# Batch 1's convolution as a step of the order, silu(z) with a place per batch, fewer root steps on GpSimd, and a new order of all engines

## What is computed

```python
# mixer: context (4,256,128), z = layernorm(x) (4,256,256)
x1 = silu(conv4(in_proj(ctx)) + conv_b)            # 256 channels
dt_low, B, C = split(x_proj(x1))                   # 8, 16, 16
dt = softplus(dt_proj(dt_low) + dt_b); A = -exp(A_log)
state = state * exp(dt*A) + (dt*x1) * B            # scan over 256 positions, 16 states a channel
y = (sum_n state*C + D*x1) * silu(z)
x = x + y
# feed-forward, on layernorm(x)
bitlinear(v, w, b) = act_quant(rms_norm(v)) @ weight_quant(w).T + b
h = gelu(silu(bitlinear(v, w1, b1)))               # 1024 wide
x = x + bitlinear(layer_norm(h, g, b), w2, b2)
```

## Time and profile before

| what | value |
|---|---|
| runs of the kernel (us) | 204.31, 201.55, 202.54; median 202.54 |
| profiled execution, span from its first to its last instruction | 201.9 us |
| its own device time | not given apart from the span; the fastest run is 0.35 us under the span, the median 0.6 us over it |
| mean granted TensorE clock | 0.890 of full speed |
| table loads on ScalarE | 28 |

### The profile page before, as it was taken

One profiled execution on the slowest core, in us unless ns is written; L12 is line 12 of the kernel. 1 busy time (PEld: TensorE's weight loads), 2 busy tenths in 40 slices (PEclk: granted clock), 3 DMA queues, 4 the chain that ended last, 5 costly groups with the idle time before them and its releaser, 6 DMA issues.

```text
span 201.9 us, 3382 instructions
## 1 busy us (share of the span) xinstructions
PE 161.6 (80%) x1161; PEld 121.8 (60%) x1167; DVE 164.1 (81%) x249; ACT 161.2 (80%) x262; POOL 142.9 (71%) x139
## 2 busy tenths in 40 slices
...
GB/s 176 292 93 364 413 419 101 3 203 206 10 208 9 97 114 0 187 220 21 148 60 0 109 104 153 58 26 0 0 3 0 0 0 26 28 28 3 11 25 70
DMA packets 20193, 20.13 MB, mean 100 GB/s; under 512 B 13448, under 2 KB 16976, under 8 KB 19536
## 3 DMA queue, kind: packets, MB, share of 16 engines
...
...
## 4 chain that ended last, share of the span: by engine, by line
ACT 24%; PE 24%; POOL 17%; DVE 17%; issue 14%; DMA 1%; DVEq 0%; POOLq 0%; ACTq 0%
ACT dA L692 10%; DVE st L1006 7%; POOL st L847 7%; PE ps L512 4%; PE ps L588 4%; PE ps L451 3%; PE ps L551 3%; DVE stats L1076 3%; PE ps L612 2%; POOL sm L874 2%; PE ps L619 2%; POOL sm L872 2%; ACT w_raw L729 2%; POOL sm L876 1%; PE ps L480 1%
## 5 line engine op out<-in xcount | busy, mean ns | idle before, releaser
L847 POOL TENSOR_TENSOR st<-st,bc 128x1024 f32<-128x1024 f32 x32 | 75.5, 2372 | 19.2 <-DVE st L1006 18.9
L1006 DVE TENSOR_TENSOR_SCAN st<-dA,ps 128x1024 f32<-128x1024 f32 x32 | 72.3, 2276 | 7.5 <-PE ps L512 6.1
L692 ACT ACTIVATE dA<-dt,negA 128x255 f32<-128x255 f32 x128 | 53.2, 498 | 0.2
L512 PE MATMUL ps<-diagB,dtuT 64*128 64x128 f32 x512 | 44.8, 306 | 4.9 <-DVE st L1006 3.5
L512 PEld LDWEIGHTS ps<-diagB,dtuT 64*128 64x128 f32 x512 | 34.9, 198 | 18.1 <-issue 9.5
L551 PE MATMUL ps<-id_f,st 128*128 128x128 f32 x256 | 35.2, 288 | 2.3 <-POOL st L847 2.3
L551 PEld LDWEIGHTS ps<-id_f,st 128*128 128x128 f32 x256 | 29.8, 147 | 5.8 <-POOL st L847 3.0
L612 PE MATMUL ps<-id_f,w_raw 128*128 128x128 f32 x64 | 11.7, 343 | 14.0 <-POOL w_raw L911 8.9
L612 PEld LDWEIGHTS ps<-id_f,w_raw 128*128 128x128 f32 x64 | 9.9, 181 | 15.4 <-issue 13.9
L588 PE MATMUL ps<-rows_sb,diag 128*128 128x512 f32 x32 | 17.2, 663 | 0.4 <-ACT w_raw L725 0.4
L761 ACT ACTIVATE q2T<-ps 128x1024 bf16<-128x1024 f32 x8 | 8.1, 1013 | 10.4 <-PE ps L612 10.4
...
## 6 DMA issues: line engine op xcount, KB each, us to landing
...
w_raw<-w2T SPq DMA_DIRECT2D x1, 1024.0 KB, 12.3
...
```

Source lines behind the costliest of these rows:

```text
L512: mm = nc.tensor.matmul(o[:, i:i + SG // 2, t, r, :], dtuT[rows, b % 2, h, t, :], diagB[rows, b % 2, t, n, :], start=True, stop=True)
L692: e = nc.scalar.activation(dA[:, k % DA_RING, i * L + 1:(i + 1) * L], dt[:, h, b % 2, 1:L], ACT.Exp, scale=negA[:, h, n:n + 1])
L847: tt(s, s, bc[:, ng].rearrange("p s l -> p (s l)"), ALU.mult).then_inc(prod_done, 1)
L1006: nc.vector.tensor_tensor_scan(st[:, k % ST_RING, :], dA[:, k % DA_RING, :], slot(k), 0.0, ALU.mult, ALU.add).then_inc(scanned, 1)
```

## The change

Batch 1's convolution, `turn_half(0)`, `scale_b(0)` and `scale_rest(0)` become steps of `PE_AT`; the first writes bank 2 instead of bank 0, batch 2's bank 3 instead of 2, with their own waits. `silu_z` writes a buffer of its own for each batch and no longer waits for `z_turned`. GpSimd's `root1` and `root2b` fold the factor 127/1e-5 into the number whose root is taken and have two steps instead of three; `root2a` leaves out its third step for tiles 4 to 7. `out_scale`, `quant1` and `wmean` use the other scale. ScalarE's table loads are written out, by the set last loaded. All four tables are new.

```diff
...
 VECTOR_AT = (
+    "z_norm:1 spread_b:1 spread_b:2 spread_b:3",
+    "dt_half:1",
+    "",
     "dt_neg:1",
+    "dt_mask:1 wmean:0",
+    "",
+    "dt_sum:1",
+    "",
+    "dt_neg:2",
     "dt_mask:2",
     "gate:0 gate:1 x1:0 x1:1",
+    "",
+    "ln1:0 dt_sum:2",
+    "quant1:0",
+    "",
+    "dt_neg:3 clip_weights:0 clip_weights:1",
+    "dt_mask:3",
+    "dt_sum:3 bn2:0",
+    "",
+    "gate:2 gate:3 x1:2 x1:3 gain:0 ln1:1",
+    "",
     "quant1:1",
+    "",
+    "amax2:0",
+    "scales2:0",
+    "bn2:1 bn2:2",
+    "gate:4 gate:5 x1:4 x1:5 gain:1",
+    "",
+    "gain:2 amax2:1 scales2:1 ln1:2",
+    "amax2:2 bn2:3 scales2:2",
+    "res:0 quant1:2 gain:3",
+    "",
+    "amax2:3 bn2:4 gain:4 scales2:3 gate:6 gate:7 x1:6 x1:7 res:1 ln1:3 res:2 quant1:3 amax2:4 bn2:5 scales2:4 "
+    "gain:5 amax2:5 bn2:6 scales2:5 gain:6 res:3 bn2:7 amax2:6 gain:7 scales2:6 res:4 amax2:7 scales2:7 res:5 "
+    "res:6 res:7",
 )
 SCALAR_AT = (
     "silu_u:1",
     "copy_xd:1",
+    "",
+    "",
+    "sum_weights:0 dt_bias:1",
+    "copy_half:1 sum_weights:1 dt_exp:1",
+    "silu_z:0 silu_u:2",
     "copy_xd:2",
+    "copy_du:1",
     "dt_bias:2",
     "dt_exp:2",
     "copy_z:0",
+    "silu_z:1 scale_weights:0 silu_u:3",
+    "copy_xd:3",
     "",
     "copy_du:2",
     "dt_bias:3",
+    "copy_q1:0",
+    "scale_weights:1 dt_exp:3",
+    "",
+    "silu:0 copy_z:1 gelu:0 silu_z:2 silu_z:3 copy_du:3 silu:1 norm:0",
+    "copy_z:2",
+    "copy_z:3 square:0",
+    "",
+    "",
+    "",
     "copy_q1:1",
+    "silu:2 gelu:1 gelu:2 scale2:0",
+    "copy_q2:0 norm:1",
+    "",
+    "norm:2 square:1 silu:3 gelu:3 scale2:1 square:2",
+    "copy_q2:1 scale2:2 norm:3 copy_q2:2",
+    "copy_q1:2 silu:4 gelu:4 square:3 silu:5 gelu:5 scale2:3 square:4 copy_q2:3 copy_q1:3 silu:6 gelu:6 "
+    "square:5 silu:7 gelu:7 square:6 copy_q2:4 copy_q2:5 square:7 copy_q2:6 copy_q2:7",
 )
 POOL_AT = (
+    "z_root:0",
+    "",
     "",
     "",
     "dt_series:1",
+    "",
+    "",
     "",
     "",
     "dt_series:2",
     "",
     "",
+    "root1:0 add_b2:0",
+    "",
+    "",
     "dt_series:3",
     "",
+    "root2a:0",
+    "",
+    "shift:0 add_b2:1 root1:1 root2b:0",
+    "",
+    "",
+    "",
+    "out_scale:0",
+    "",
+    "root2a:1 root2a:2",
+    "shift:1",
+    "root2b:1 shift:2 out_scale:1 root1:2",
+    "root2b:2 root2a:3",
+    "",
     "shift:3",
     "",
+    "root2a:4 root2b:3 add_b2:2 out_scale:2 out_scale:3 root1:3 add_b2:3 root2b:4 out_scale:4 root2a:5 "
+    "scale_last:4 root2b:5 root2a:6 out_scale:5 scale_last:5 root2a:7 root2b:6 scale_last:6 root2b:7 "
+    "scale_last:7 out_scale:6 out_scale:7",
 )
 PE_AT = (
+    "convolve:2 convolve:3 turn_half:0 xdbl:1 scale_b:0 scale_rest:0 scale_b:1 dtraw:1 convolve:4 scale_b:2 "
+    "scale_rest:1 scale_rest:2 convolve:5",
+    "turn_half:1 scale_b:3 scale_rest:3 scale_b:4 scale_rest:4",
+    "wsum:0",
+    "scale_b:5 scale_rest:5",
+    "scale_b:6 xdbl:2 scale_rest:6 scale_b:7 scale_rest:7 turn_du:1",
+    "dtraw:2 scale_b:8 scale_rest:8",
+    "scale_b:9 scale_rest:9",
+    "turn_z:0 scale_b:10",
+    "scale_rest:10 scale_b:11 scale_rest:11 convolve:6 convolve:7",
+    "scale_b:12 xdbl:3 scale_b:13",
+    "scale_rest:12",
+    "turn_du:2",
+    "scale_rest:13 scale_b:14 dtraw:3 scale_rest:14 turn_q1:0",
+    "scale_b:15 scale_rest:15 scale_b:16 scale_rest:16 turn_z:1 bias:0",
+    "",
+    "mm1:0 scale_b:17 scale_rest:17 bias:1 scale_b:18",
+    "scale_rest:18 turn_du:3 mm1:1 turn_z:2 scale_b:19 scale_rest:19 scale_b:20 scale_rest:20",
+    "turn_z:3",
+    "",
+    "scale_b:21 scale_rest:21 scale_b:22 scale_rest:22 turn_q1:1",
+    "bias:2 scale_b:23 scale_rest:23 mm1:2",
+    "scale_b:24 scale_rest:24 scale_b:25 scale_rest:25",
+    "",
+    "",
+    "turn_q2:0 scale_b:26 scale_rest:26 scale_b:27 bias:3 scale_rest:27",
+    "mm1:3 scale_b:28 scale_b:29 scale_rest:28 scale_rest:29",
+    "",
+    "mm2:0 turn_q2:1 scale_b:30 scale_rest:30",
+    "turn_q2:2 scale_b:31 scale_rest:31 turn_q1:2 bias:4 mm1:4 bias:5",
+    "mm1:5",
+    "",
+    "",
+    "mm2:1 mm2:2 turn_q2:3 turn_q1:3 bias:6 mm1:6 mm2:3 bias:7 turn_q2:4 mm1:7 turn_q2:5 mm2:4 mm2:5 turn_q2:6 "
+    "turn_q2:7 mm2:6 mm2:7",
 )
...
         def xin(b):
-            return bank(0) if b == 1 else bank(2)
+            return bank(3) if b == 2 else bank(2)
...
-            held = {"big": (diagB_done, GROUPS), "low": (scanned, UNITS - 1), "high": (scanned, UNITS)}
+            held = {"big": (u_ready, NB), "low": (scanned, UNITS - 1), "high": (scanned, UNITS)}
...
                 if i == HALVES:
                     pe.wait_ge(in_ctx, 16)
                     pe.wait_ge(taps_scaled, 1)
-                elif h == 0:
-                    take("big", u_ready, b + 1)
+                    pe.wait_ge(u_ready, 1)
+                elif i == 2 * HALVES:
+                    pe.wait_ge(diagB_done, GROUPS)
+                elif i == 3 * HALVES:
+                    pe.wait_ge(u_ready, 2)
...
             b_cols()
-            for i in range(HALVES, 2 * HALVES):
-                convolve(i)
-            pe.wait_ge(in_id, 16)
-            turn_half(0)
-            scale_b(0)
-            scale_rest(0)
...
             def silu_z(b):
                 act.wait_ge(z_small, 4)
-                if b:
-                    act.wait_ge(z_turned, b)
                 for h in range(HALVES):
                     j = h * NB + b
-                    nc.scalar.activation(siluz[:, h, :], x_nat[:, h, b, :], ACT.Silu,
+                    nc.scalar.activation(siluz[:, b, h, :], x_nat[:, h, b, :], ACT.Silu,
...
             def root2a(t):
...
-                pool.wait_ge(root2a_step, 3 * t + 2)
-                ts(s[:, 2:3], mv2[:, t % 2, 0:1], s[:, 1:2], -1.0, ALU.mult, ALU.mult).then_inc(root2a_step, 1)
+                if t < LAST:
+                    pool.wait_ge(root2a_step, 3 * t + 2)
+                    ts(s[:, 2:3], mv2[:, t % 2, 0:1], s[:, 1:2], -1.0, ALU.mult, ALU.mult).then_inc(root2a_step, 1)
...
             def root2b(t):
...
-                tt(s[:, 5:6], s[:, 4:5], m_half[:, 0:1], ALU.pow).then_inc(root2b_step, 1)
-                pool.wait_ge(root2b_step, 3 * t + 2)
-                ts(s[:, 6:7], s[:, 5:6], LEVELS / EPS, None, ALU.mult).then_inc(root2b_step, 1)
+                tt(s[:, 6:7], s[:, 4:5], m_half[:, 0:1], ALU.pow).then_inc(root2b_step, 1)
...
+            dt_neg(0)
             z_norm(0)
-            dt_neg(0)
...
```

More of the change, by code:

```diff
@@ L54 @@
 VECTOR_AT = (
-    "spread_b:1 spread_b:2 dt_half:1",
-    "spread_b:3",
+    "z_norm:1 spread_b:1 spread_b:2 spread_b:3",
+    "dt_half:1",
+    "",
     "dt_neg:1",
+    "dt_mask:1 wmean:0",
     "",
-    "z_norm:1 dt_mask:1 wmean:0 dt_sum:1",
+    "dt_sum:1",
     "",
-    "dt_neg:2 clip_weights:0",
+    "dt_neg:2",
     "dt_mask:2",
+    "gate:0 gate:1 x1:0 x1:1",
+    "",
[8 more added lines that the diff above has]
+    "",
+    "quant1:1",
+    "",
[11 more added lines that the diff above has]
+    "res:6 res:7",
+)
+SCALAR_AT = (
+    "silu_u:1",
+    "copy_xd:1",
+    "",
[3 more added lines that the diff above has]
+    "silu_z:0 silu_u:2",
+    "copy_xd:2",
+    "copy_du:1",
+    "dt_bias:2",
+    "dt_exp:2",
+    "copy_z:0",
+    "silu_z:1 scale_weights:0 silu_u:3",
+    "copy_xd:3",
+    "",
+    "copy_du:2",
+    "dt_bias:3",
+    "copy_q1:0",
[4 more added lines that the diff above has]
+    "copy_z:3 square:0",
     "",
@@ L65 @@
     "",
-    "gate:0 gate:1 x1:0 x1:1",
-    "dt_sum:2 ln1:0",
-    "quant1:0 dt_neg:3 clip_weights:1",
-    "",
[L70 to L89, removed]
-)
[L91 to L102, removed]
+    "copy_q1:1",
+    "silu:2 gelu:1 gelu:2 scale2:0",
+    "copy_q2:0 norm:1",
+    "",
+    "norm:2 square:1 silu:3 gelu:3 scale2:1 square:2",
+    "copy_q2:1 scale2:2 norm:3 copy_q2:2",
+    "copy_q1:2 silu:4 gelu:4 square:3 silu:5 gelu:5 scale2:3 square:4 copy_q2:3 copy_q1:3 silu:6 gelu:6 "
+    "square:5 silu:7 gelu:7 square:6 copy_q2:4 copy_q2:5 square:7 copy_q2:6 copy_q2:7",
+)
+POOL_AT = (
+    "z_root:0",
     "",
@@ L105 @@
     "",
[L106 to L111, removed]
-    "",
-    "",
[L114 to L127, removed]
-POOL_AT = (
-    "",
-    "",
-    "dt_series:1",
-    "z_root:0",
+    "dt_series:1",
+    "",
+    "",
     "",
@@ L167 @@
-    "scale_rest:3 convolve:5",
-    "scale_b:4 scale_b:5 wsum:0 scale_rest:4 scale_rest:5 xdbl:2",
-    "turn_du:1",
-    "convolve:6 scale_b:6 dtraw:2 scale_b:7 scale_rest:6 scale_rest:7",
-    "convolve:7",
-    "",
-    "turn_z:0 scale_b:8 scale_rest:8 scale_b:9 scale_rest:9",
-    "scale_b:10 scale_rest:10 scale_b:11",
-    "scale_rest:11 scale_b:12 xdbl:3",
-    "",
-    "scale_rest:12 turn_du:2 scale_b:13 dtraw:3",
-    "scale_rest:13 scale_b:14 turn_q1:0 bias:0 scale_rest:14",
-    "mm1:0 turn_z:1 scale_b:15 scale_rest:15",
@@ L539, in sum_states @@
                         pe.wait_ge(diag_D_done, HALVES)
-                        pe.wait_ge(u_ready, 2)
                     elif h == 0:
```

126 lines of the change are left out of this document (48 added, 78 removed).

## The result

The changed kernel takes 217.88 us (median of four runs, 215.45 to 218.88) against 202.56 us; the ratio is 1.0706, with a 95% interval of 1.061 to 1.080. Every ratio here is one of means, taken without the runs that lie over 1.5% above the fastest of their kernel, and so differs a little from the quotient of the medians (1.0756 here). The forecast was 195.0 us. The direction was wrong, and the time lies outside the range.

A forecast was written before the change was run, and what follows sets the result against it. No engine alone was taken as the bound; the order decides, with everything hanging from VectorE's 32 scans. Span 201.9 - 4.5 - 2.1 - 0.9 = 194.4 us, plus 0.6 gives a forecast of 195.0 us, range 190.0 to 201.5.

The forecast's parts named there:

- The new order of the scans: First to last scan: the reordered tables cut VectorE's waits, its work unchanged at 119.5 us; 4.5 us saved.
- Its standing: VectorE's waits between scans: 6.4 us instead of 10.9, of which 1.8 us allowed for handovers.
- the small steps: Root steps on GpSimd: long ones are held up beside VectorE's two-input instructions, so the next small step would be too.
- The cold clock: Rival: TensorE stands in rows 16 to 23 and its clock falls, 9.4 us lost, run 204.4; chance 0.07.
- ScalarE ahead of `bn2:0`: Rival: late ScalarE holds `bn2:0`, scan 17 and all behind it; gain only 3.5 us, run 199.0; chance 0.22.
- Start: Before the first scan: moving batch 1's convolution gains nothing; scan 0 at 24.1 us, as before.
- Loads: ScalarE's table loads: 26 instead of 28, 2.6 us off ScalarE.
- Root steps: GpSimd's shorter root steps on the chain of the end: 1.4 us counted, 0.9 taken; 2.9 if the long times were their own.
- After the last scan: ScalarE's last row: earlier pieces bring tile 6's `silu` to +15.9 us from +18.9; 2.1 of 3 us taken.
- From span to run: Whole kernel: 0.6 us added to the span, which stood that far below the runs' median of 202.54.
- the sum: Whole span: 201.9 less 4.5 (scans), 2.1 (after the last scan) and 0.9 (root steps) gives 194.4 us.

The follow-up runs named there:

- e10: e1 with GpSimd's step `root1:0` moved behind the product of unit 11 instead of in front of it; 202.74 us, ratio 0.9904.
- e1: The changed kernel's new code with all four tables of the kernel before (the old order); 199.74 us, ratio 0.986 to the kernel before.
- e3: The changed kernel with GpSimd's product by C left out and four one-column powers in its place; 191.91 us, ratio 0.9465.
- e4: The changed kernel with each GpSimd product cut into four instructions of 128x256; 207.88 us, ratio 1.0246.
- e5: The changed kernel with four groups of GpSimd's steps put in front of their products; 217.18 us, ratio 1.0665.
- e6: The kernel before with the change's shorter root steps alone; 200.53 us, ratio 0.9838.

## Why the prediction was wrong

- **The step that failed** is the first of "The new order of the scans": "VectorE's work up to the last scan is the same set in both orders (119.5 us)". The set is the same and its time is not. From the first scan to the last scan's end VectorE was busy 118.4 us before and 143.4 us after. A duration from the trace of before was a duration in that order, with GpSimd kept away. The hand count put each product at the end of its scan, beside the side steps, and took both at their lengths. What the runs show in its place: a meeting with a product under way adds up to 2.1 us to a VectorE instruction (2.0 in e10), 24.4 us in the whole kernel, and goes with the order (e1) and with the products (e3).
- **Its standing was forecast well**: 6.4 us expected between scans, and VectorE's timeline after has waits of 1.86, 0.21, 1.28, 0.83 and 1.12, 5.3 us. What made the scans late was the stretches: scan 6 starts at 49.41 instead of the forecast 44.5, and L959, L1139 and L972 ahead of it took 2.0, 1.8 and 2.0 us too much.
- **The prediction had the mechanism in its hand**, and only for the small steps: "I read this as GpSimd held up, so the next small step will be held up in its place." It worked in one direction. The opposite one, VectorE held up by a product of 2.37 us, was never asked. The trace of before had a row of the opposite direction, beside a smaller GpSimd instruction:

```profile
163.62 1.27 POOL L864 TENSOR_TENSOR x_nat<-x_nat,rows_sb 128x512 f32<-128x512 f32 x1
...
164.05 1.26 DVE L1041 TENSOR_SCALAR xc<-x_nat,mv 128x256 f32<-128x256 f32 x2
```

The two instructions of L1041 take 0.62 us together elsewhere (136.90). The Trainium skill's sentence (GPSIMD Engine Reference, its opening table: the SBUF interfaces are shared with VectorE) names no direction; e10's trace agrees, with 2.0 us for one meeting (L971).
- **No rival was it.** The cold clock, the one on the slower side, came in part, as a consequence: from 98 to 130 us, its rows, the granted clock was 0.79, so in part at the lower of its two levels (before, from 80 to 121 us, 0.96); TensorE's products waited for scans 12 times in the whole kernel, 13.9 us. It did not make the loss: VectorE's timeline lists no wait between 65 and 134 us, and the mean clock is 0.890 in both. ScalarE ahead of `bn2:0` did not hold scan 17 up; VectorE itself was late.
- **Start**: right, 24.08 us, and batch 1's convolution gained nothing. The number is in part luck: e3, e4 and e5 have the same start and scan from 22.45 us on. TensorE's granted clock from 13 to 20 us, during this convolution, was 0.76 in them and 0.54 here (0.59 in the kernel before). Why it differs stays open; e1's span has 1.5 us from it.
- **Loads**: right in number. 26 table loads, 2.6 us off ScalarE, in the order where they were not the limit.
- **Root steps**: the mechanism was right, the term too small. 0.9 us forecast, 3.0 measured (e6).
- **After the last scan**: 43.0 us against 44.5 forecast, 4.5 us saved where 3.0 were expected. Root steps make up 3.0 of it. That leaves 1.4 us for the new order, forecast as 2.1, and not on the way described: `silu` of tile 6 comes 18.0 us after the last scan's end, forecast 16, before 18.9.
- **From span to run**: the forecast added 0.6 us. A run's time stands 1.9 us above its own span (218.88 and 217.0); the 0.6 was the distance from one execution's span to the median of others.

Without the products the kernel takes 191.9 us (e3), a span of 190.3 against the 194.4 of the sum; 1.6 of these 4.1 us are the start's clock and, by e6, 2.1 the root steps. So the count was good but for the stretches: this span is 26.7 us shorter than the changed kernel's, and VectorE is busy for 24.7 us less in it.
